# Shift before scores on TensorE, exponentials first on ScalarE, in the two attention loops of a decoder layer

## The reference

```python
scores = jnp.einsum('sbhd,tbhd->bhst', q * scale, k)      # self-attention
attn = jax.nn.softmax(scores, axis=-1)                     # over the keys
out = jnp.einsum('bhst,tbhd->sbhd', attn, v)
...
scores = jnp.einsum('nhtd,nhsd->nhts', qh, kh) / jnp.sqrt(jnp.float32(HID))   # cross-attention
attn = jax.nn.softmax(scores, axis=1)                      # over the HEADS
out = jnp.einsum('nhts,nhsd->nhtd', attn, vh)
...
topv, topi = jax.lax.top_k(weights, TOP_K)                 # 3 of 15 experts for each row
return shared_enc + router_enc + x
```

## Time and profile before

| | |
|---|---|
| runs of the kernel before | 363.4, 366.54, 366.6 us (median 366.54) |
| the profiled execution | 363.38 us, span 361.6 us |
| busy share of the span | PE 73%, DVE 61%, POOL 59%, ACT 52% |
| first loop, steps 0 to 15 | about 13 to 73 us |
| second loop, first to last maxima | 100.5 to 162.8 us |
| scatter to the experts | 175.3 to 239.4 us |

### The profile page before, as it was taken

How to read it: one execution, slowest core, us unless ns; L and a number is a source line. 1 busy time by engine, 2 the same in 40 slices (tenths; PEclk the granted TensorE clock), 3 DMA queues, 4 the chain that set the end, 5 groups by cost and what they waited for, 6 DMA issues and landing times.

```text
span 361.6 us, 6474 instructions
## 1 busy us (share of the span) xinstructions
PE 263.3 (73%) x2031; PEld 202.5 (56%) x2031; DVE 218.9 (61%) x578; ACT 188.1 (52%) x391; POOL 213.4 (59%) x219
## 2 busy tenths in 40 slices
PE   3889899883369787673699699949999898910700
PEld 1778889682234344341567486539998787810200
DVE  5568798983177899989273706634666555400550
ACT  2589698342546769442353704306887676720050
POOL 4526556695515455425778777734777777772380
PEclk9999999998586999985589959987999999975565
DMA  7973001002790000000011112423443333213612
GB/s 234 402 155 56 4 0 31 12 21 58 223 383 14 2 2 0 3 1 2 22 60 37 47 58 82 132 61 81 120 120 108 101 101 107 79 54 116 255 44 72
DMA packets 38194, 31.28 MB, mean 87 GB/s; under 512 B 12960, under 2 KB 31408, under 8 KB 37776
## 3 DMA queue, kind: packets, MB, share of 16 engines
q1 hardware_dynamic: 32448, 21.08, 19.9%
q0 software_dynamic: 3520, 7.27, 5.9%
q10 hardware_dynamic: 2192, 2.52, 2.3%
HBM read 19.38 MB, written 11.47 MB: 85 GB/s over the span
## 4 chain that ended last, share of the span: by engine, by line
POOL 28%; PE 20%; issue 18%; DVE 15%; ACT 10%; DMA 7%; SPq 0%; ACTq 0%; DVEq 0%; POOLq 0%
POOL x_srt L1487 13%; POOL y_tok L1507 5%; DMA y_tok<-k_heads,y_rows 3%; POOL v_pairs L1450 3%; PE psum L767 3%; PE psum L758 3%; ACT q_heads L882 3%; PE psum L557 3%; DVE prob_sums L1162 3%; DVE maxes L1156 3%; ACT q_heads L807 2%; PE psum L458 2%; DMA v_pairs<-y_tok 1%; DMA bias_cols<-b_col 1%; PE psum L543 1%
## 5 line engine op out<-in xcount | busy, mean ns | idle before, releaser
L1507 POOL DMA_INDIRECT y_tok<-k_heads,y_rows x62 | 61.6, 994 | 27.3 <-issue 16.5
L1487 POOL DMA_INDIRECT x_srt<-v_blocks,slot x48 | 47.2, 982 | 14.3 <-issue 14.3
L1456 POOL TENSOR_TENSOR k_heads<-k_heads,inv_sums 128x1024 f32<-128x1024 f32 x16 | 30.9, 1934 | 40.4 <-DVE inv_sums L1167 40.4
L988 ACT ACTIVATE k_heads<-psum,k_heads 128x128 f32<-128x128 f32 x124 | 38.7, 366 | 17.0 <-PE psum L758 14.3
L767 PE MATMUL psum<-k_heads 128*128 128x128 f32 x248 | 40.9, 288 | 4.8 <-ACT k_heads L988 4.0
L758 PE MATMUL psum<-k_heads 128*128 128x128 f32 x248 | 39.2, 282 | 0.0
L767 PEld LDWEIGHTS psum<-k_heads 128*128 128x128 f32 x248 | 33.3, 195 | 8.8 <-ACT k_heads L988 8.4
L1369 DVE COPY k_heads<-psum 128x128 f32<-128x128 f32 x62 | 18.1, 292 | 28.9 <-PE psum L750 28.4
L758 PEld LDWEIGHTS psum<-k_heads 128*128 128x128 f32 x248 | 33.9, 198 | 0.0
L557 PE MATMUL psum<-q_heads,k_heads 64*64 64x256 f32 x256 | 20.6, 444 | 15.6 <-ACT k_heads L891 9.3
L996 ACT ACTIVATE k_heads<-psum,k_heads 128x128 f32<-128x128 f32 x62 | 22.9, 369 | 16.2 <-DMA y_tok<-k_heads,y_rows 14.5
(11 more groups left out here) (159 smaller groups left out, 588.1 us busy)
## 6 DMA issues: line engine op xcount, KB each, us to landing
expert_w<-e_w SPq DMA_DIRECT2D x1, 4369.0 KB, 16.3
k_heads<-x_srt SPq DMA_DIRECT2D x62, 65.0 KB, 1.9
x_srt<-pad SPq DMA_DIRECT2D x16, 65.0 KB, 2.8
xT<-x_t SPq DMA_DIRECT2D x4, 256.0 KB, 6.9
x_rows<-x_n SPq DMA_DIRECT2D x1, 1024.0 KB, 9.4
ctxT_k<-ctx_k SPq DMA_DIRECT2D x1, 1024.0 KB, 12.0
ctxT_v<-ctx_v SPq DMA_DIRECT2D x1, 1024.0 KB, 13.7
v_scr<-v_rows SPq DMA_DIRECT2D x4, 256.0 KB, 6.4
```

The lines of the kernel that those rows point to most:

```text
L988: ins = act.activation(h_tile[:, t % 2, a, :], bank[2 + t % 2][:, P * a:P * a + P], ACT.Gelu, bias=stage[:, t % NS, EW - 2 + a:EW - 1 + a])
L1456: pool.tensor_tensor(probs2[:, p % 3, :].rearrange("p (t h) -> p t h", t=B), probs2[:, p % 3, :].rearrange("p (t h) -> p t h", t=B), inv_s ...
L1487: pool.indirect_dma_start(out=x_srt, out_offset=bass.IndirectOffsetOnAxis(ap=slot[:, n:n + 1], axis=0), in_=payloads[:, g, k, :], in_offse ...
L1507: pool.indirect_dma_start(out=y_tok, out_offset=bass.IndirectOffsetOnAxis(ap=y_rows[:, t:t + 1].bitcast(mybir.dt.uint32), axis=0), in_=y_t ...
```

## The change

In both loops, PE's step `i` now does the shift of portion `i` before the scores of portion `i+1`. In the second loop the shift also stands ahead of `weighted2(i-3)` and of `proj_cq`. ACT's step in the second loop now begins with `exps2(i)`, ahead of the copies `u2_out(i-3)` and of `q_masked2`. No instruction is added or removed, and DVE, POOL and SP keep their order.

```diff
@@ PE, first loop
                 if i == 0:
                     scores(0)
+                if i < NG:
+                    subtract_max(i)
                 if i + 1 < NG:
                     scores(i + 1)
                 if i == 0:
                     proj_v(2)
-                if i < NG:
-                    subtract_max(i)
@@ PE, second loop
             for i in range(STEPS2):
+                if i < NP:
+                    subtract_max2(i)
                 if 3 <= i < NP + 3:
                     weighted2(i - 3)
                 if i % PAIRS == 0 and i // PAIRS + 1 < OCT:
                     proj_cq(i // PAIRS + 1)
                 if i + 1 < NP:
                     scores2(i + 1)
-                if i < NP:
-                    subtract_max2(i)
@@ ACT, second loop
             for i in range(STEPS2):
+                if i < NP:
+                    exps2(i)
                 if 3 <= i < NP + 3:
                     u2_out(i - 3)
                 if i % PAIRS in (1, 2) and i // PAIRS + 1 < OCT:
                     q_masked2(i // PAIRS + 1, range(2 * (i % PAIRS) - 2, 2 * (i % PAIRS)))
-                if i < NP:
-                    exps2(i)
```

## The result

| | before | after |
|---|---|---|
| median of 6 runs each | 363.98 us (361.7 to 366.6) | 372.0 us (371.25 to 372.8) |
| ratio, 95% interval | | 1.021 (1.0159 to 1.026) |
| the profiled execution, its span | 363.38, 361.6 us | 371.9, 370.1 us |
| mean granted clock | 0.862 | 0.864 |

The change costs 8.0 us, and the predicted 373.0 us lies 1.0 above the median. Part of that nearness is luck: the forecast added 6.7 us to 366.54, the median of the three runs then known, while over six runs the median of before is 363.98. The cost itself was forecast at 6.7 us and is 8.0.

What follows compares the result with a forecast made beforehand. PE was taken to bound the first loop, DVE the second, POOL what follows. First loop +1.2 and second loop +5.5 (3.9 plus 1.6 for the clock) make +6.7 on 366.54, so 373 us; range 366.8 to 377.

Steps and rivals of the forecast that it cites:

- The first loop: First loop: PE stands idle for DVE's maxima once scores follow the shift; +1.2 us, between 0 and 1.5.
- the first shift: First loop, first portion: PE waits for the maxima with no scores to run meanwhile; 0.93 us.
- step 4: First loop, fifth step: the shift would again wait for the maxima; 0.3 to 0.55 us.
- The ring: Second loop: maxima, shift, weighted sums, next scores, next maxima in one chain; 3.94 us, 5.03 with a projection; +3.9 in all.
- The clock: Second loop's opening: PE idle about 2.5 us may drop to 1.2 GHz; +1.6 us, between nothing and 3.55.
- 0→1: Second loop, maxima of portion 0 to those of portion 1: 2.70 us before, 5.09 worked out, +2.39.
- 2→5: Second loop, maxima of portion 2 to those of portion 5: 11.72 us before, 11.87 worked out, +0.15.
- The slow-clock rival: Second loop: PE at 1.2 GHz for most of it, seven plain steps paying 1.3 us more; 382 us; chance 10%.
- the faster rival: Second loop: scores slip in early, DVE's 3.1 us of waits for exponentials vanish, nothing replaces them; 363.4 us; chance 7%.
- the hidden one: Second loop: DVE's bookkeeping and sliding work cover the loss, only the first loop's term is left; about 367.7 us; 13%.
- Exponentials first: Second loop, ACT: moving exponentials to the head of a step gives nothing, since they also wait for weighted sums.
- One for one to the end: Behind the second loop: POOL's scatters follow without slack, so a delay at either loop's end reaches the program's end in full.

## Why the prediction was right, and the term that was mis-sized

**The first loop** was forecast at 1.2 and cost 1.40. Its terms were 0.93 for the first shift (0.92 by the run without it) and 0.3 to 0.55 for step 4 (0.50 for all others together; the wait of 0.44 stands at 28.92). Step 3 has a new wait of 0.27 us, which takes the place of one of 0.52. The later steps, put at zero, are zero: L441 is 30.93 - 29.45 = 1.48 late, 0.11 of it from the start, and the loop as a whole ends 1.40 late.

**The ring** was the mechanism, and the runs show it three ways. PE's move without ACT's gives the loss (69.77 of 70.15 us). Its members add up: plain steps took 3.95 and 4.02 us against 3.94 worked out, a projection step 5.06 against 5.03, 6→9 13.03 against 12.91, 13→14 4.67 against 4.7. And with the weighted sums and the projection taken out of it, it has 2.98 us. From 9 to 13 DVE's own work hides it, 17.40 against 17.33. The 1→2 step, put at zero, cost 0.13.

**The clock** is the mis-sized term. I took 1.6 us, with 3.55 as the upper bound; it was about 3.7. 0→1 took 6.00 where 5.09 had been worked out with the scores of portion 1 at full clock: those scores ran at 1.2 GHz too, 0.9 us. (The projection at 1.2 GHz takes 1.84 us from start to start and not 1.68, because the 1.75 of the earlier trace rows is a row in which the clock came up; the shift takes 0.83 and not 0.97, and the two nearly cancel.) 2→5 took 14.69 where 11.87 had been worked out: 2.8 us. The busy PE ahead of the loop brings that stretch to 12.05 in the changed kernel, which is the shown cause. I had reasoned from a single pause of about 2.5 us, as if one pause put the clock down and busy steps brought it back; in this execution the pause is not there, each step of the opening has one of 1.35 us, and 1.2 GHz lasts from ahead of 99.98 to 122 us. With PE's move alone the pause of 2.48 us is there as foreseen, the clock is up ahead of it and falls behind it, and by the same count the term is 0.5 + 2.3 = 2.8 us. So the size of this term changes with the execution, by about 1 us in these two, and a single trace gives it only so well. With 3.7 the loop's 7.87 us lie just above its range of 3.9 to 7.5.

**The slow-clock rival** had the place wrong. It saw the clock low in the plain steps through most of the loop; there it is up (0.97 from 123 us on), pauses of 1.35 us in every step or not. The Trainium skill, "TensorE: Matmul & The Clock Gate", section "A second HAM failure mode: psum-queue depth-cycling", has frequent short idles make the clock go back and forth. From 123 us on the trace does not bear that out, with 0.97; in the opening, with idles of the same length, the clock stays down at 0.52. No run here tells what makes the difference.

**Matmuls in program order.** No row of after shows scores ahead of a waiting shift; the shift's 14 waits on the maxima all hold PE. That agrees with the rule cited from the Trainium skill, "PSUM — Partial Sum Buffer", and the faster rival, which needed the opposite, is gone. Gone too is the hidden one: DVE's bookkeeping hides the ring only from 9 to 13, in the last step (5.89 us in both) and nearly in those with query rows (1→2 and 5→6).

**Exponentials first** was said to give nothing, and in the changed kernel it gave nothing (70.15 with it, 69.77 without). Alone it is neutral in time as well, ratio 0.9974 (0.9929 to 1.002), and in the trace it costs, for a reason that I had not seen: it takes 1.1 and 0.7 us off two intervals and hands 1.2 and 2.1 to those in which the query cuts are late.

**One for one to the end** holds within 0.9 us: 9.38 at the first scatter, 8.5 in the span. "Near 181" for the first scatter was 3.6 us short of 184.64. The prediction's own sum would have been 175.26 + 6.7 = 181.96; of the 2.68 us beyond it 2.1 is the clock, 0.2 the first loop, 0.11 the start and the rest small terms of the loop.

## What to carry to other kernels

On an engine that works in order, an instruction that waits for another engine puts everything behind it into one ring with that engine: before moving a wait to the head of a step, add up the ring from start to start and compare it with the bottleneck engine's own work in each kind of step. Issue the next portion's producer ahead of the waiting instruction, and keep unrelated work out of the ring. Where TensorE idles for several us ahead of a stretch bound by such turn-arounds, matmuls that only keep it busy can pay: here 18 of them took 3.4 us (1.0%) off the kernel before. They helped where they ended 0.9 to 1.6 us ahead of the first scores; behind a wait of 1.8 us the clock fell again, in one run of the old order and in the changed kernel.

## What was unexpected of the hardware

- Pauses of one length did not always leave the clock alike. In the changed kernel with PE kept busy first, it fell behind pauses of 1.78 and 1.35 us with 1.09 us of scores between them; from 123 us on the same 1.35 us pauses, with two to three groups between them, left it at 0.97.
- In the opening of the changed kernel the clock was 0.52 for 21 us in which PE was busy 14.53 us. With PE's move alone, the same list of PE instructions in the second loop had the clock back after 9 us, at 107.63, and lost it again.
- The kernel before took 362 to 367 us on two chips and 395 to 410 on two others. The kernel with the 18 matmuls was traced on one of either kind: the first scatter is at 172.36 and 172.50 us, the last at 236.04 and 243.79, POOL waits 8.16 and 22.28 us ahead of the first gather, and the last gather is at 324.36 and 366.22. So the 42 us all lie behind the attention loops, most of them in the part of experts and gathers. The slower one was traced at 402.42 us, and the fastest executions there took 393.25 and 394.36, so some 33 of the 42 us are left between the chips. The cause is open.
